# A graph layer on one core: two pauses per histogram group, and a first block without GpSimd's reduction and without a clearing of semaphores

## The reference

```
h   = x * rsqrt(deg_out)
m   = segment_sum(h[src], dst) * rsqrt(deg_in)
x1  = m @ W_gc + b_gc + x @ W_res + b_res
y   = x1 + moe(x1)          # 64 experts, top 2, 256 -> 512 -> 256, gelu
z   = batch_norm(y) * gamma + beta
out = layer_norm(x + z)
```

## Time and profile before

| | |
|---|---|
| median of 3 runs | 3221.69 us |
| lowest, highest | 3211.83, 3242.91 us |
| profiled execution, its own time | 3230.26 us |
| its span, first to last instruction | 3228.5 us |
| mean granted TensorE clock, share of full speed | 0.934 |
| PE busy | 2649.7 us, 82% |
| DVE busy | 2058.5 us, 64% |
| ACT busy | 1246.1 us, 39% |
| POOL busy | 2088.2 us, 65% |
| DMA over the span | 653.48 MB, 202 GB/s |

### The profile page before, as it was taken

One profiled execution on the slowest core, in us unless ns is written; L12 is line 12 of the kernel. 1 busy time (PEld: TensorE's weight loads), 2 busy tenths in 40 slices (PEclk: granted clock), 3 DMA queues, 4 the chain that ended last, 5 costly groups with the idle time before them and its releaser, 6 DMA issues. The chain is left out here.

```text
span 3228.5 us, 60318 instructions
## 1 busy us (share of the span) xinstructions
PE 2649.7 (82%) x14863; PEld 2041.7 (63%) x14993; DVE 2058.5 (64%) x7326; ACT 1246.1 (39%) x2934; POOL 2088.2 (65%) x2142
## 2 busy tenths in 40 slices
PE   4661889989988999989898988888959999999650
PEld 4551556556665665656776767677648888889640
DVE  7994456656665666657666666666555555555698
ACT  4992122223222222323333333333324444444339
POOL 6877677777777777777777777777715555555300
PEclk8875899999999999999999999999979999999885
DMA  7569545455455554556887787777766555654477
GB/s 255 164 205 352 169 142 177 146 191 178 144 181 168 164 178 147 178 189 186 259 247 249 238 252 232 254 247 227 225 229 190 176 184 180 188 175 137 150 290 250
DMA packets 415795, 653.48 MB, mean 202 GB/s; under 512 B 70847, under 2 KB 307165, under 8 KB 413938
## 3 DMA queue, kind: packets, MB, share of 16 engines
q1 hardware_dynamic: 299790, 355.25, 33.8%
q0 software_dynamic: 101712, 273.85, 28.3%
q10 hardware_dynamic: 14100, 22.04, 1.9%
HBM read 515.73 MB, written 139.19 MB: 203 GB/s over the span
## 5 line engine op out<-in xcount | busy, mean ns | idle before, releaser
L1586 POOL DMA_INDIRECT work<-h_table,src_cols x1452 | 1382.3, 952 | 454.2 <-issue 427.7
L2158 PE MATMUL ps<-work 128*128 128x257 f32 x3322 | 1003.0, 396 | 139.0 <-DMA work<-h_table,src_cols 126.9
L2158 PEld LDWEIGHTS ps<-work 128*128 128x128 f32 x3322 | 575.7, 192 | 392.9 <-issue 268.6
L2309 POOL DMA_INDIRECT picked<-ys,places x160 | 171.5, 1072 | 268.1 <-DVE ys L2386 249.4
L2446 PEld LDWEIGHTS ps<-xst,work 128*128 128x128 f32 x2560 | 310.4, 193 | 28.8 <-issue 17.4
L2446 PE MATMUL ps<-xst,work 128*128 128x128 f32 x2560 | 315.9, 277 | 12.2 <-issue 11.4
L1986 PE MATMUL ps<-none_w,none 128*128 128x512 bf16 x815 | 312.3, 383 | 0.0
L2453 PE MATMUL ps<-work,hid 128*128 128x256 f32 x1280 | 306.9, 383 | 2.5 <-ACT hid L2288 1.0
L2288 ACT ACTIVATE hid<-ps,b_cols 128x128 f32<-128x128 f32 x640 | 219.0, 367 | 117.0 <-PE ps L2446 85.1
L2453 PEld LDWEIGHTS ps<-work,hid 128*128 128x128 f32 x1280 | 230.8, 190 | 35.6 <-ACT hid L2288 10.1
L1611 DVE TENSOR_TENSOR work<-rel_cols,ps 128x1152 f32<-128x1152 f32 x196 | 250.3, 1278 | 4.2 <-PE ps L2158 4.0
(11 more groups left out here) (373 smaller groups left out, 5023.7 us busy)
## 6 DMA issues: line engine op xcount, KB each, us to landing
acc<-in_L_gnn_w_dram SPq DMA_DIRECT2D x136, 512.0 KB
work<-in_L_gnn_w_dram SPq DMA_DIRECT2D x128, 512.0 KB
picked<-work SPq DMA_DIRECT2D x14, 1792.0 KB, 8.7
work<-x_ahead SPq DMA_DIRECT2D x182, 128.0 KB
pk<-picked SPq DMA_DIRECT2D x13, 1792.0 KB, 10.0
work<-h_table,src_cols POOLq DMA_INDIRECT x1452
acc<-m_base SPq DMA_DIRECT2D x14, 903.0 KB, 6.7
x_beta<-xr_x SPq DMA_DIRECT2D x98, 128.0 KB
```

Of the source, the lines that this page charges most:

```text
L1586: pool.indirect_dma_start(out=got[:, c % RING, 0:D], out_offset=None, in_=h_table[:, :], in_offset=bass.IndirectOffsetOnAxis(ap=src_cols[: ...
L2158: mm = nc.tensor.matmul(ps_flat[:, bank(t, k, w[0])], hot[:, (2 * t + (k >= HALF)) % HOTS, k % HALF if k >= HALF else k, :], got[:, c % RI ...
L2309: pool.indirect_dma_start(out=picked[:, :], out_offset=bass.IndirectOffsetOnAxis(ap=places[:, u:u + 1], axis=0), in_=ys[:, u, :], in_offse ...
```

## The change

VectorE pauses twice in each group of the histogram: after the two upper codes it waits for a new semaphore that the second of them raises (highs_made), and after the two lower codes it waits for hot_ready, which it raises itself. In the first block the clearing of semaphores with its meeting of the queues is left out, so the block's semaphores keep their numbers and values. TensorE multiplies the one column vmax with the identity, which gives it as a row in PSUM; VectorE reduces this row to the flag. GpSimd has no reduction any more. SOONEST is 11: GpSimd fetches 11 chunks of early rows in the first block, and 16 in the second.

```diff
-SOONEST = 8
+SOONEST = 11
...
-            with nc.cleanup_on_exit(), ExitStack() as part:
+            with ExitStack() as part:
...
+                vmax_turned = sem2("vmax_turned")
...
                         nc.vector.tensor_tensor(vmax[:, :], vmax[:, :], vpace[:, :], ALU.max).then_inc(vmax_set, 1)
+                        dve.wait_ge(vmax_turned, 1)
+                        nc.vector.tensor_reduce(vall[0:1, :], ps[0:1, 1, 0:P], AX_X, ALU.max).then_inc(vall_set, 1)
                         dve.wait_ge(vall_set, 1)
...
-                        pool.wait_ge(vmax_set, 1)
-                        nc.gpsimd.partition_all_reduce(vall[:, :], vmax[:, :], P,
-                                                       bass.bass_isa.ReduceOp.max).then_inc(vall_set, 1)
                         pool.wait_ge(early_x_in, 16 * SOONEST)
...
                         nc.tensor.transpose(ps[:, 0, 0:READY], rows_ef[:, :], ident[0:READY, 0:READY]).then_inc(early_turned, 1)
+                        pe.wait_ge(vmax_set, 1)
+                        nc.tensor.matmul(ps[0:1, 1, 0:P], vmax[:, 0:1], ident[:, :], start=True, stop=True).then_inc(vmax_turned, 1)
...
+        highs_made = sem2("highs_made")
...
                         hi, hi_values = codes_and_values(hi_b, NT, a, b)
-                        nc.vector.tensor_tensor(hot_hi[:, k, a:b, :, :], hi, hi_values, ALU.is_equal)
+                        last = nc.vector.tensor_tensor(hot_hi[:, k, a:b, :, :], hi, hi_values, ALU.is_equal)
+                    last.then_inc(highs_made, 1)
+                    dve.wait_ge(highs_made, g + 1)
                     for a, b in ((0, WHOLE // 2), (WHOLE // 2, WHOLE)):
                         lo, lo_values = codes_and_values(lo_b, P, a, b)
                         last = nc.vector.tensor_tensor(hot_lo[:, k, a:b, :, :], lo, lo_values, ALU.is_equal)
                     last.then_inc(hot_ready, 1)
+                    dve.wait_ge(hot_ready, g + 1)
```

## The result

| | before | changed |
|---|---|---|
| median | 3222.63 us (7 runs) | 3240.02 us (7 runs) |
| lowest, highest | 3209.95, 3242.91 us | 3238.80, 3244.06 us |
| profiled execution, its own time | 3230.26 us | 3244.06 us |
| span | 3228.5 us | 3242.3 us |
| second block left by all queues | 334.0 us | 342.7 us |

The changed kernel is slower by 0.6%: ratio 1.0063, interval 1.0034 to 1.0092. It is also steady, 5 us from lowest to highest, where the kernel before spreads over 33 us.

A forecast was written before the change was run, and what follows sets the result against it. GpSimd's staging chain was taken to bound the second block; its 28.3 us gain would hide behind a store chain 47 us later, leaving -3.8 us: 3226.5 us from the profiled 3230.3, forecast 3225 us, range 3206 to 3242 us.

The forecast's parts named there:

- the two pauses: VectorE's histogram, second block: 0.47 us a group, 49 us over 104 groups; bounds 24 and 62 us.
- rival C: Histogram loop: pauses dear, 0.6 us a group, 62 us, branch and counter exposed after the second pause; 3233 to 3239 us, chance 0.14.
- The ordinary pause: One wait in VectorE's histogram: 0.08 us of lost overlap plus 0.16 us of gap, taken as 0.235 us.
- The loop's turn: Histogram loop's branch and counter, about 0.1 us every second group, counted only in the highest price of 0.6 us a group.
- Rivals A and B: Histogram pauses: A cheap, 24 us in all, 3213 us, chance 0.18; B free, -28.3 us, 3202 us, chance 0.05.
- The first block: Gain 1.5 us from dropping GpSimd's reduction, 0.6 us from semaphores not cleared; all queues start the second block 2.0 us earlier.
- the configuration: GpSimd's pool configuration, no longer switched back before the second block's first IOTA: 7 us more for GpSimd, 9 in all.
- The long fetch: GpSimd's staging, second block: one fetch shrinks from 22.76 to 0.95 us because pauses give GpSimd openings; 21.8 us gained.
- The store chain: h_table's stores, second block: first at 283.3 us, 350 GB/s once alone, landed at 329.8 us, closing the block at 330.0.
- From the profiled execution to the median: The old median lies 8.6 us below the profiled execution; the sum of 3226.5 us was therefore lowered to 3225 us.
- One to one behind the block: After the second block nothing changes, so what the first 335 us gain or lose passes on one to one.
- D: Staging: the long fetch stays, not held by VectorE; stores land 6.6 us later than before, 3237 us, chance 0.11.

The follow-up runs named there:

- c_p1: The changed kernel with only the first pause of each group, after the upper codes, without the wait on hot_ready: 3223.2 us, ratio 1.0020 to the kernel before.
- e_k0: The changed kernel with one pause only every second group, after the upper codes of even groups: 3211.0 us, ratio 0.9972 to the kernel before.
- f_turn4: The changed kernel with VectorE's histogram loop turning every four groups instead of two, both pauses kept: 3233.1 us, ratio 1.0045 to the kernel before.
- b_first: The changed kernel without its two pauses, so only the first block's change: 3217.6 us, ratio 0.9996 to the kernel before.
- k_ring4: The changed kernel without pauses and with a ring of four stages in place of eight, so GpSimd waits longer: 3256.6 us, one run.

## Why the prediction was wrong, point by point

The step that failed is "the two pauses", its price of 0.47 us a group and 49 us in all. It was 63.1 us (298.0 against 234.9 us with the pauses taken out), 0.61 us a group, just above the end that I had given as highest. The outcome is rival C, in its mechanism (the turn of the loop laid bare by the second pause) and within 1 us of its time (3233 to 3239 us forecast, 3240.0 measured); I had given it 0.14.

- *The ordinary pause.* 0.235 us each was forecast, 0.22 to 0.23 measured (c_p1, e_k0). The row from the experts' loop was the right one to take.
- *The loop's turn.* The bound held 0.1 us every second group, from the branch's 0.056 us and the counter. Measured: a gap of 0.51 us at the turn against 0.15 elsewhere, 0.36 us, and f_turn4 took 26 turns away for 8.2 us (0.32 each). 51 turns are 16 to 18 us, more than the 14.1 us that were missing; the ordinary pauses were a little cheaper than forecast. The sequencer's durations in the earlier trace rows are not what a turn costs once nothing is queued ahead on the engine; why it takes 0.2 to 0.3 us more than the 0.1 us of the bound isn't shown.
- *Rivals A and B fall.* No pause was cheap, none free. The page "VectorE: DVE Perf Modes" of the Trainium skill (section "The DRAIN you can't avoid") says that the semaphore costs nothing extra; here the same two lines with a wait between them stand 0.20 us further apart, and 104 such waits moved the first store by 22.7 us.
- *The first block.* 2.0 us for VectorE forecast, 1.1 measured, since the eleventh fetch took 2.9 us to land and drain. GpSimd's first IOTA: 8.2 us earlier, 9 forecast; behind the block's earlier start that leaves 7.1 us for the configuration, priced at 7, though no run takes the reduction out alone. The loads and the wait for a stage: 5.5 and 7.0 us earlier, 6.5 forecast for both.
- *The long fetch* vanished, as forecast, but the forecast's reason isn't shown: the wait ended with the clock at half, where b_first's fetch was short without any pause. Staging ended 21.7 us earlier, not 28.3 (last fetch 304.36 against 297.8 us), since the fetches beside the paused histogram came more slowly: 165 intervals of 1.36 us in place of 1.32.
- *The store chain.* It took the block's end over, as forecast. 350 GB/s alone was taken, 347 measured. The stores landed 44.4 us after the first was issued; the forecast had 46.5 (283.3 to 329.8). With 63.1 us in place of 49 the same sum closes the block at 337.3 us, 7.3 of the 12.7 us that it was late. A second term was too small as well: the stores had the engines alone from 317.7 us on, not from 303.8. Beside the staging, from 298 to 318 us, h_table moved 4.72 MB, 236 GB/s and not 183. Put in with the first block's 0.9 us, they bring the same sum to about 341.5 us, an estimate from these rates, 1.2 before the measured end.
- *From the profiled execution to the median.* I let the forecast sink towards the median of before. But the long fetch was in that median too. Half of the executions lie in the upper group, and the three profiled executions of this kernel and of b_first that do so have a long fetch, so the old median is most likely a mixture, and the changed kernel, bound by its stores, gains nothing from its absence. This moved the forecast 1.5 us the wrong way.
- *One to one behind the block.* Held: 2899.6 us remained against 2894.5, inside the 2892 to 2900 of all profiles.

What D asked is answered in part. Five fetches were long, each behind a wait of GpSimd's, and beside each VectorE ran without a break: four times its histogram, once its scaling. The four ended 0.86 to 0.89 us behind VectorE's first late start, the fifth 0.8 us behind the scaling's end, at a clock of 0.50. That fits VectorE's histogram and scaling holding GpSimd until a gap or their end, and a clock that matters only because its fall makes such gaps; it is an inference from these five endings. The Trainium skill, page "SBUF — State Buffer", section "Who interferes with whom", names two-input instructions as contending with GpSimd's reads. No run here shows which port was held; if it was VectorE that held GpSimd, it did so for 15 to 31 us beside two-input instructions, that is 9 to 18 groups, and once beside a scaling with one tensor input.

Left open: whether a pause frees GpSimd where TensorE's clock is full. In none of the seven profiles with pauses and such a wait did the wait end at a settled full clock. That 78 timed runs of kernels with pauses lie within 9 us of each other, kernel by kernel, doesn't settle it, nor is it shown why a fetch that follows on another isn't held, or why the three of k_ring4 from 266 to 272 us were not.

## What to carry to other kernels

Before adding a wait to an engine whose sequencer runs ahead, look for what comes next in its queue: the pause with an address register behind it left a gap of 0.12 to 0.15 us here, the one at the loop's turn 0.51 us. When a median hides two populations, find the event that separates them, and see which step triggers it; here moving two loads behind the first stores took away the wait that led to it and was worth more than slowing the engine beside it. And where a stall sits on one of two chains that end close together, removing it is worth only the distance to the other, which the cure must not lengthen.

## What the runs showed of the hardware that I had not expected

- A GpSimd fetch issued after an idle time beside a gapless VectorE histogram took 15.1, 17.7, 22.8 and 31.4 us in place of 0.95, in four profiles. All four began with TensorE's granted clock at 1.00 (2.4 GHz) and ended 3.5 to 3.6 us after it had fallen to 0.50 (1.2 GHz), 0.86 to 0.89 us after VectorE's first late start, when its period went from 1.76 to 1.78-1.82 us. A fifth, of 5.9 us beside VectorE's scaling, stood at 0.50 from start to end. The 104 to 138 fetches beside each unpaused histogram that followed on one another took 0.94 to 1.33 us at either level.
- Without GpSimd's reduction and the clearing behind it, the next block's first GpSimd instruction came 8.2 us earlier, far more than the reduction's own 0.38 us.
- With both pauses the granted clock stood at 0.50 from 150 to 280 us, with 871 matmuls in 130 us; without them it changed between the levels.
